# Attention steps in periods of two, and projections of the next pass on row halves, in a post-norm transformer layer on 8 cores

## The chip, the cores and the metric

The kernel runs on all 8 cores of one Trainium2 chip. The time is device microseconds of the slowest core. Before the change the median of 3 runs is 1495.09 us (1491.83 to 1698.76). Each core takes half of the query blocks of one of 4 batch entries: 2048 of 4096 tokens, in 128-token blocks that alternate between two cores. There is no communication between cores.

## The reference

One layer on x of shape (4, 4096, 1024), f32, all of it computed on the chip:

```python
x = _layernorm(x + attn(x, Wq, Wk, Wv, Wo))        # 16 heads of 64, causal softmax
x = _layernorm(x + ffn(x, w_gate, w_up, w_down))   # 3072 hidden, silu(gate) * up, int weights / 127
```

Attention is `softmax(scale * Q K^T, causal) V` for each head, with Q, K and V projected from x.

## The kernel before, in words

**Attention** takes two heads per pass, 8 passes. A core's 2048 queries are 4 banks of 512; a bank is done against the key blocks that it may see, one *step* per 128 keys (in the masked part two blocks share a step): 5, 13, 21 and 29 steps, 68 per pass and 544 in all. A step is:

- `scores` (L497): K block times Q bank for head 0 on rows 0 to 63 and head 1 on rows 64 to 127 of TensorE, into one of two buffers `sps` (two PSUM banks each). The two matmuls of such a pair run at once. They wait for the exponential of two steps before.
- the exponential (L505) on ScalarE over both heads, 128x1024, into `pt`, with the pass's bound `cbias` in place of a running maximum. `masks` (L522, L529) on VectorE multiplies the diagonal blocks.
- `values` (L553): V (with a column of ones for the row sums) times `pt`, added into `ops`, one bank per head. The 128 keys are split in two halves of 64 rows: in each *phase* the two heads take different row halves, and in the second phase they swap. Since both phases add to the same banks from different rows, phase 1 waits for phase 0 (`wait(pe, s_pe, pv_at[j])`).

The order is written out: values(j-1, 0), scores(j+2), masks(j), values(j-1, 1), then filler. At a bank's end `unit_out` copies `ops` to `ostg` (L569), and the next bank's first values wait for it; 6 steps later `unit_recip` takes the reciprocal of the row sums, with a DMA before and two behind it; 16 steps later `unit_scale` (L594) multiplies, into `ofm`. These stand in VectorE's one queue with everything else there.

**Filler** is the work of the next pass, a generator that yields its cost in units of one 512-column matmul. It has 8 groups of K (`k_group`, L260), 4 of Q (L278), each 8 matmuls of 128 rows by 512 columns into one of two PSUM banks `pp`, evacuated by VectorE; 8 groups of V (L299, 16 matmuls of 256 columns each) in passes 0 to 5; and the *bound*: squares of K and Q (L328), their column sums on TensorE with a 32-column weight (`norms`, L337), a maximum (L342), `spread` and `gather_max` (L359), then `roots` on ScalarE, which give `cbias`. Credit grows by `rate` per step, and filler is issued once 4 units are saved up (2 at a bank's end): about 5 matmuls after every second step. Groups take the two banks in turn. Pass 7 has no filler.

Before attention the projections of pass 0 run from x, which is loaded by DMA. In the first 36 x 13 steps DMAs convert the feed-forward weights to bf16 in DRAM, and in pass 7 the output weights and x are loaded (L617, L621). After attention come the output projection, layer norm, gate and up, down, and the second norm.

Of the kernel before, what the change touches and what calls it, by code (L numbers as in the profile page):

```python
# [75 lines left out]
def build_program(cfg):  # L76
# [37 lines left out]
    with st:  # L114
# [128 lines left out]

        pp_free = [0, 0]
# [71 lines left out]

        sq_free = [0]
# [60 lines left out]
        def bound(p):  # L378

            squares(p, 0)  # L380
            yield 0.5
            norms(p, 0)
            squares(p, 1)
            yield 1.5
            norms(p, 1)
            squares(p, 2)
            yield 1.5
            norms(p, 2)
            spread(p)
            yield 1.5  # L390
            gather_max(p)
            yield 0.5
            roots(p)
            yield 0.0

        def together(groups, stages):

            for g in groups:
                yield from g
                cost = next(stages, None)  # L400
                if cost is not None:
                    yield cost
            for cost in stages:
                yield cost

        def proj_kq(p):
            for ts in range(NTS):
                yield from k_group(p, ts)
                if ts % 2 == 1:
                    yield from q_group(p, ts // 2)  # L410
            if p + 2 < NPASS:
                wait(pool, s_pe, s_pe.n)
                load_wk(p + 2)
                load_wq(p + 2)

        def filler(p):

            if p + 1 >= NPASS:
                return
            v = (p + 2) // 2  # L420
            yield from proj_kq(p + 1)
            groups = []
            if 2 * v < NPASS:
                lo = 0 if p % 2 == 0 else NTS // 2
                groups = [v_group(v, ts, h) for ts in range(lo, lo + NTS // 2) for h in range(2)]
            yield from together(groups, bound(p + 1))
            if p % 2 == 1 and v + 1 < NPASS // 2:
                wait(pool, s_pe, s_pe.n)
                load_wv(v + 1)

        def filler_cost(p):
            if p + 1 >= NPASS:
                return 0.0
            cost = 12 * 8 + 5.5
            if 2 * ((p + 2) // 2) < NPASS:
                cost += 8 * 16 * 0.52
            return cost
# [18 lines left out]
        load_wq(2)  # L456
        squares(0, 1)
# [7 lines left out]
        spread(0)  # L465
        gather_max(0)
# [42 lines left out]
        def masks(j):  # L509
# [9 lines left out]
            if stride == 1:  # L519
                tv = t.rearrange("p (h q) -> p h q", h=2)[:, :, 0:128]  # L520
                mv_ = m[:, 0:256].rearrange("p (h q) -> p h q", h=2)
                s_dve.inc(dve.tensor_mul(tv, tv, mv_))  # L522
            else:
                for h in range(2):
                    n = 512 // 128
                    tv = t[:, h * 512:(h + 1) * 512].rearrange(
                        "p (b q) -> p b q", b=n)[:, 0:n:stride // 128, :]
                    mv_ = m[:, h * 256:(h + 1) * 256].rearrange("p (b q) -> p b q", b=2)
                    s_dve.inc(dve.tensor_mul(tv, tv, mv_))  # L529
            pt_at[j] = (s_dve, s_dve.n)  # L530

        def values(j, phase):
# [5 lines left out]
            if phase == 0:  # L538
# [5 lines left out]
            else:  # L544

                wait(pe, s_pe, pv_at[j])
            flip = (phase + j) % 2
            for kb, q0, w, so in s["segs"]:
                for half in range(2):
                    h = half ^ flip  # L550
# [5 lines left out]
                                   start=(s["first"] and phase == 0),  # L556
                                   stop=(s["last"] and phase == 1),
# [65 lines left out]
        work = filler(0)  # L623
        credit = [0.0]
        rate = [filler_cost(0) / 66.0]

        def fill(least):
            if credit[0] < least:
                return
            while credit[0] > 0:  # L630
                cost = next(work, None)
                if cost is None:
                    credit[0] = 0.0
                    return
                credit[0] -= cost

        scores(0)
        scores(1)
        NJ = len(plan)
        for j in range(NJ + 1):  # L640
            if j > 0:
                values(j - 1, 0)
            if j + 2 < NJ:
                s = plan[j + 2]
                if s["opens"]:
                    for _ in work:
                        pass
                    p = s["p"]
                    work = filler(p)
                    rate[0] = filler_cost(p) / 66.0  # L650
                    credit[0] = 0.0
                scores(j + 2)
            if j < NJ:
                masks(j)
            if j > 0:
                values(j - 1, 1)
                done = plan[j - 1]
                if done["last"]:
                    u = done["unit"]
                    unit_out(u, j - 1)  # L660
                    pending.append((j + 6, lambda u=u: unit_recip(u)))
                    pending.append((j + 16, lambda u=u: unit_scale(u)))
                    pending.sort(key=lambda e: e[0])
                if done["p"] < NPASS - 1:
                    if j % 13 == 12:
                        convert_piece()
                else:
                    n = j - 1 - (NJ - 68)
# [299 lines left out]
```

How the kernel before makes its waits and increments, by code:

```python
    def inc(self, instr, k=1):  # L50
        instr.then_inc(self.h, k)
        self.n += k
        return self.n
# [2 lines left out]
def wait(engine, sem, value):  # L56
    if value > 0:
        engine.wait_ge(sem.h, value)
```

## Time and profile before

| | |
|---|---|
| median of 3 runs | 1495.09 us |
| the profiled execution | 1492.57 us; span of its slowest core 1491.5 us |
| cores | 1483.7 to 1491.5 us |
| TensorE matmuls busy | 1361.2 us, 91% |
| TensorE weight loads busy | 630.2 us, 42%, beside the matmuls |
| ScalarE busy | 725.3 us, 49% |
| VectorE busy | 472.8 us, 32% |
| chain that ended last | PE 81%, DVE 5%, DMA 5%, issue 5%, ACT 4% |

Busy time is the union of an engine's instructions; matmuls are pipelined, so one's duration is longer than its distance to the next, and the distances are what tells TensorE's pace. A row of the timeline gathers like instructions that follow each other: start, time from the first start to the last end, engine, line, names, count, and in brackets the idle time before and what ended it. Since rows of one engine overlap at their ends, cost is read from one row's start to the next row's start. All times below are of the slowest core, 3, from its first instruction.

### The profile page before, as it was taken

Reading aid. Unit: us, or ns where it says so; the run is one execution under the profiler, and the core shown is the slowest. Engines: PE = TensorE matmul, PEld = TensorE weight load, DVE = VectorE, ACT = ScalarE, POOL = GpSimd, SP = SyncE. Lnnn points to the kernel's source line nnn. Section 1 sums busy time; section 2 is a strip of 40 time slices with the busy share of each in tenths; the row PEclk is TensorE's granted clock in tenths of the full one; section 3 lists DMA queues with packets and bytes.
Section 4 is the critical chain, followed back from the end, with each engine's and each line's share of the span. In section 5 each row is a group of like instructions: output and inputs, shape, how many; then the busy total and the mean of one; then the engine's idle time right before and its main releaser. Section 6 shows DMA issues by size and latency. Waiting matters only on the chain.

```text
span 1491.5 us, 23901 instructions; the slowest of 8 cores (1483.7 to 1491.5 us)
## 1 busy us (share of the span) xinstructions
PE 1361.2 (91%) x8432; PEld 630.2 (42%) x8432; DVE 472.8 (32%) x950; ACT 725.3 (49%) x809; POOL 97.8 (7%) x190
## 2 busy tenths in 40 slices
PE   5989999999999999999997687889999999999998
PEld 3634434434434444434433333334444444444443
DVE  1432333333334333332423125622231222122222
ACT  0067666766776676666786793641101121130123
POOL 2000000000000000000000110011101101100100
PEclk9999999999999999999998899999999999999999
DMA  9913113222122223221321641038304423431422
GB/s 153 152 26 50 37 35 52 44 51 51 30 51 36 53 42 51 44 36 22 54 48 30 160 137 64 1 114 268 127 15 147 153 82 114 153 130 58 154 85 99
DMA packets 38863, 119.68 MB, mean 80 GB/s; under 512 B 13280, under 2 KB 13280, under 8 KB 36576
## 3 DMA queue, kind: packets, MB, share of 16 engines
q0 software_dynamic: 24096, 100.68, 28.7%
q1 hardware_dynamic: 14656, 17.47, 3.7%
q8 instruction: 76, 1.25, 0.3%
q14 instruction: 35, 0.29, 0.1%
HBM read 145.13 MB, written 27.39 MB: 116 GB/s over the span
## 4 chain that ended last, share of the span: by engine, by line
PE 81%; DVE 5%; DMA 5%; issue 5%; ACT 4%; POOL 0%; DVEq 0%; ACTq 0%; SPq 0%; POOLq 0%
PE ops L553 20%; PE gps L816 11%; PE ups L822 11%; PE dps L876 11%; PE sps L497 7%; PE pp L260 7%; PE pp L299 7%; PE pp L278 3%; DMA xb<-xP 3%; ACT pt L505 2%; PE dps L728 2%; DVE ostg L569 2%; DMA linvd<-rcol 1%; DVE vbuf L311 1%; DMA lb<-linvd 1%
## 5 line engine op out<-in xcount | busy, mean ns | idle before, releaser
L505 ACT ACTIVATE pt<-sps,cbias 128x1024 bf16<-128x1024 f32 x544 | 575.8, 1117 | 235.2 <-PE sps L497 229.8
L553 PE MATMUL ops<-pt,vbuf 64*65 64x512 bf16 (+3 forms) x2560 | 397.9, 361 | 49.4 <-DVE ostg L569 18.7
L553 PEld LDWEIGHTS ops<-pt,vbuf 64*65 64x65 bf16 x2560 | 150.2, 106 | 297.3 <-issue 293.7
L828 ACT ACTIVATE sgb<-gps 128x512 bf16<-128x512 f32 x96 | 57.3, 597 | 371.3 <-PE gps L816 371.3
L497 PE MATMUL sps<-qbuf,kbuf 64*128 64x512 bf16 (+3 forms) x1280 | 220.2, 353 | 10.8 <-ACT pt L505 9.7
L816 PE MATMUL gps<-x1T,wgu 128*128 128x512 bf16 x768 | 183.2, 382 | 0.0
L822 PE MATMUL ups<-x1T,wgu 128*128 128x512 bf16 x768 | 181.9, 380 | 0.0
L876 PE MATMUL dps<-wd,hbuf 128*128 128x512 bf16 x768 | 166.4, 379 | 0.0
L260 PE MATMUL pp<-xb,wkb 128*128 128x512 bf16 x512 | 134.4, 391 | 19.2 <-DMA xb<-xP 18.3
L831 DVE SCALAR_TENSOR_TENSOR hbuf<-ups,sgb 128x512 bf16<-128x512 f32 x96 | 66.4, 692 | 267.3 <-PE ups L822 267.3
L299 PE MATMUL pp<-wvb,xb 128*128 128x256 bf16 x1024 | 133.2, 277 | 12.2 <-DVE vbuf L311 12.1
L299 PEld LDWEIGHTS pp<-wvb,xb 128*128 128x128 bf16 x1024 | 94.5, 99 | 47.6 <-issue 34.6
L816 PEld LDWEIGHTS gps<-x1T,wgu 128*128 128x128 bf16 x768 | 75.5, 98 | 91.3 <-issue 1.7
L822 PEld LDWEIGHTS ups<-x1T,wgu 128*128 128x128 bf16 x768 | 75.3, 98 | 91.3 <-issue 1.1
L876 PEld LDWEIGHTS dps<-wd,hbuf 128*128 128x128 bf16 x768 | 75.1, 98 | 90.6
L267 DVE CAST kbuf<-pp 128x512 bf16<-128x512 f32 x64 | 44.2, 691 | 183.9 <-PE pp L260 183.9
L497 PEld LDWEIGHTS sps<-qbuf,kbuf 64*128 64x128 bf16 x1280 | 77.0, 101 | 50.4 <-issue 41.5
L311 DVE CAST vbuf<-pp 128x512 bf16<-128x512 f32 x64 | 44.4, 694 | 168.5 <-PE pp L299 168.5
L770 POOL DMA_DIRECT2D wgu<-wgub x96 | 50.6, 528 | 492.7 <-PE ups L822 476.8
L260 PEld LDWEIGHTS pp<-xb,wkb 128*128 128x128 bf16 x512 | 43.9, 99 | 80.6 <-issue 43.9
L278 PE MATMUL pp<-xb,wqb 128*128 128x512 bf16 x256 | 68.3, 384 | 0.0
L884 DVE SCALAR_TENSOR_TENSOR x<-x,mv,dps 128x512 f32<-128x512 f32 x32 | 23.9, 748 | 114.3 <-PE dps L876 102.2
(55 smaller groups left out, 594.9 us busy)
## 6 DMA issues: line engine op xcount, KB each, us to landing
wgu<-wgub POOLq DMA_DIRECT2D x96, 512.0 KB, 4.3
wgub<-wguP POOLq DMA_DIRECT2D x24, 512.0 KB, 6.2
xb<-xP POOLq DMA_DIRECT2D x8, 1024.0 KB, 38.2
lb<-linvd SPq DMA_DIRECT2D x32, 256.0 KB, 3.7
x<-xtok POOLq DMA_DIRECT2D x16, 512.0 KB, 4.3
yout<-x SPq DMA_DIRECT2D x15, 512.0 KB, 2.7
wdb<-wdP POOLq DMA_DIRECT2D x12, 512.0 KB, 6.1
wd<-wdb POOLq DMA_DIRECT2D x6, 1024.0 KB, 8.5
```

Of the source, the lines that this page charges most:

```text
L260: mm = pe.matmul(pp[i][:, :], wkb[p % 2][:, c * 128:(c + 1) * 128], xb[ts][:, c * 512:(c + 1) * 512], start=(c == 0), stop=(c == NCH - 1))
L278: mm = pe.matmul(pp[i][:, :], wqb[p % 2][:, c * 128:(c + 1) * 128], xb[2 * g][:, c * 512:(c + 1) * 512], start=(c == 0), stop=(c == NCH - 1))
L299: mm = pe.matmul(pp[i][:, b * 256:(b + 1) * 256], xb[ts][:, c * 512 + t0:c * 512 + t0 + 128], wvb[v % 2][:, c * 256:(c + 1) * 256], start= ...
L311: s_dve.inc(dve.tensor_copy(dst, src))
L497: mm = pe.matmul(buf[:, h * 512 + so:h * 512 + so + w], kt[r, kb * 128:kb * 128 + 128], qt[r, g * 512 + q0:g * 512 + q0 + w], start=True, ...
L505: exp_at[j] = s_act.inc(act.activation(pt[j % NPT][:, :], buf[:, :], AF.Exp, bias=cbias[p % 2][:, 0:1]))
L553: mm = pe.matmul(ops[:, h * 512 + q0:h * 512 + q0 + w], vt[r, c0:c0 + 65], pt[j % NPT][r, h * 512 + so:h * 512 + so + w], start=(s["first" ...
L816: mm = pe.matmul(gps[:, :], wgu[i][:, c * 128:(c + 1) * 128], xt[:, c * 512:(c + 1) * 512], start=(c == 0), stop=(c == NCH - 1))
L822: mm = pe.matmul(ups[j][:, :], wgu[i][:, D + c * 128:D + (c + 1) * 128], xt[:, c * 512:(c + 1) * 512], start=(c == 0), stop=(c == NCH - 1))
L828: gps_free[0] = s_act.inc(act.activation(sgb[j][:, :], gps[:, :], AF.Silu, scale=QS))
L831: h_at[hc] = s_dve.inc(dve.scalar_tensor_tensor(hbuf[:, hc * 512:(hc + 1) * 512], ups[j][:, :], QS * QS, sgb[j][:, :], op0=ALU.mult, op1=A ...
L876: mm = pe.matmul(dps[i][h][:, :], hbuf[:, hc * 512 + k * 128:hc * 512 + k * 128 + 128], wd[:, hc * D + h * 512:hc * D + h * 512 + 512], st ...
```

## The change

1. *Periods of two steps.* Steps of one bank are taken two at a time. A period is: the second halves of the values of the two steps before (one wait for both), then for each of its own steps scores two ahead, mask, and the first half of its values, then filler. Which head is on which rows now depends on the period. A bank has an odd number of steps, so its last period has one.
2. *Projections on row halves.* Groups of filler go in pairs, as `kq_pair` and `v_quad`: a matmul of 128 rows becomes two of 64, one for each group (and each `pp` bank), on different rows at the same time. After 8 such pairs the groups turn: each takes the other half of its rows, and waits for the first turn. Both banks must be free before a pair of groups starts, and both are evacuated behind it. The code before the passes keeps its 128-row groups.
3. *Filler kept for bank ends.* Each bank gets its share per period, less 7.5 units, which are issued between the scores and the first values after a bank's end. Filler stops at a turn or at a group pair's end, except that at a bank's end it goes past a turn. The stages of the bound are spread over the filler at other places, and the first K pair of pass 1 is issued before `gather_max` of pass 0 (`ahead`).
4. *Masks* in the strided case are one VectorE instruction in place of two.

```diff
+        def halves(outs, lhs, rhs, turns, first, last):
+            for half in range(2):
+                n = half ^ turns
+                r = slice(64 * half, 64 * half + 64)
+                mm = pe.matmul(outs[n], lhs[n][r, :], rhs[n][r, :], start=first, stop=last)
+            return mm
+        def kq_pair(p, w, w_sem, w_value, tiles, evacuate):
+            for i in range(2):
+                wait(pe, s_dve, pp_free[i])
+                wait(pe, s_xb[tiles[i]], 16)
+            wait(pe, w_sem, w_value)
+            for turns in range(2):
+                if turns == 1:
+                    wait(pe, s_pe, flipped)
+                for c in range(NCH):
+                    wc = w[:, c * 128:(c + 1) * 128]
+                    mm = halves([pp[0][:, :], pp[1][:, :]], [wc, wc],
+                                [xb[t][:, c * 512:(c + 1) * 512] for t in tiles],
+                                turns, turns == 0 and c == 0, turns == 1 and c == NCH - 1)
...
+                                wait(dve, s_pe, flipped)
+                                pp_free[i] = evacuate(i)
+                    yield 1.0
+                yield FLIP if turns == 0 else DONE
...
+        def v_quad(v, ts):
...
+            for b, turns in ((0, 0), (0, 1), (1, 1), (1, 0)):
+                opening = (b == turns)
+                if not opening:
+                    wait(pe, s_pe, flipped)
...
+        def fill(least, over_flips=False):
+            if credit[0] < least:
+                return
+            while credit[0] > 0:
+                cost = next(work, None)
...
+                if cost > 0:
+                    credit[0] -= cost
+                elif cost == DONE or not over_flips:
+                    return
...
         spread(0)
+        ahead()
         gather_max(0)
...
+        for n, now in enumerate(periods):
+            heads = n % 2
+            if before:
+
+                wait(pe, s_pe, pv_at[before[-1]])
+            for j in before:
+                values(j, 1, heads)
+                finished(j)
...
+                share = max(0.0, rate[0] * steps - AT_END) / ((steps + 1) // 2)
+            for j in now:
+                look_ahead(j + 2)
                 masks(j)
+                if plan[j]["first"] and j > 0:
+                    credit[0] += AT_END
+                    fill(0.1, over_flips=True)
+                values(j, 0, heads)
+                settle(j)
+            credit[0] += share
+            fill(1.0)
+            before = now
```

TensorE's order in pass 0, in its fourth bank, where V is the filler (`ops` are values, `sps` scores, `wvb` the V weights; the number behind `pt` is the buffer, so the step). Before:

```order
L299 MATMUL pp<-wvb_73,xb_45 128x256 x9
L553 MATMUL ops<-pt_96,vbuf_80 65x512 x2
L497 MATMUL sps<-qbuf_78,kbuf_76 128x512 x2
L553 MATMUL ops<-pt_96,vbuf_80 65x512 x2
L553 MATMUL ops<-pt_97,vbuf_80 65x512 x2
L497 MATMUL sps<-qbuf_78,kbuf_76 128x512 x2
L553 MATMUL ops<-pt_97,vbuf_80 65x512 x2
L299 MATMUL pp<-wvb_73,xb_45 128x256 x7
```

Now, in the same bank:

```order
L324 MATMUL pp<-wvb_73,xb_45 128x256 x16
L640 MATMUL ops<-pt_98,vbuf_80 65x512 x2
L640 MATMUL ops<-pt_95,vbuf_80 65x512 x2
L592 MATMUL sps<-qbuf_78,kbuf_76 128x512 x2
L640 MATMUL ops<-pt_96,vbuf_80 65x512 x2
L592 MATMUL sps<-qbuf_78,kbuf_76 128x512 x2
L640 MATMUL ops<-pt_97,vbuf_80 65x512 x2
L324 MATMUL pp<-wvb_73,xb_46 128x256 x16
```

The two halves of one step, which stood on either side of one scores, now have the filler between them; the second halves of two steps stand together. A filler row of 16 is 8 pairs.

TensorE's order at the end of the third bank of pass 0 (the last step is the one of 256-column values). Before:

```order
L278 MATMUL pp<-xb_49,wqb_71 128x512
L299 MATMUL pp<-wvb_73,xb_43 128x256 x7
L553 MATMUL ops<-pt_97,vbuf_80 65x256 x4
L497 MATMUL sps<-qbuf_78,kbuf_76 128x512 x2
L553 MATMUL ops<-pt_97,vbuf_80 65x256 x4
L299 MATMUL pp<-wvb_73,xb_43 128x256 x5
L553 MATMUL ops<-pt_98,vbuf_80 65x512 x2
L497 MATMUL sps<-qbuf_78,kbuf_76 128x512 x2
```

Now:

```order
L592 MATMUL sps<-qbuf_78,kbuf_76 128x512 x2
L640 MATMUL ops<-pt_97,vbuf_80 65x256 x4
L324 MATMUL pp<-wvb_73,xb_43 128x256 x16
L640 MATMUL ops<-pt_97,vbuf_80 65x256 x4
L592 MATMUL sps<-qbuf_78,kbuf_76 128x512 x2
L324 MATMUL pp<-wvb_73,xb_43 128x256 x26
L640 MATMUL ops<-pt_98,vbuf_80 65x512 x2
L592 MATMUL sps<-qbuf_78,kbuf_76 128x512 x2
```

Between the bank's last values and the next bank's first stood 5 matmuls of 256 columns; now there are one scores pair and 13 pairs of 256 columns. The first values stand ahead of the scores in the one, and behind one of them in the other.

## Rows read from the trace of the kernel before

**Rows 1.** Cores: span and mean granted clock, the slowest and the fastest.
```profile
core 3: 1491.5 us, clock 0.977
core 4: 1483.7 us, clock 0.980
```

**Rows 2.** Busy time by stretch; from 78.10 on one row for a pass.
```profile
78.10:181.70 103.60, 97.86 (x700) 43.98 (x700) 34.13 (x74) 72.43 (x70) 3.58 (x7) 0.97 0.21 34
...
288.50:394.60 106.10, 98.98 (x721) 45.03 (x718) 37.67 (x82) 72.77 (x71) 3.89 (x8) 0.98 0.26 46
...
711.50:808.10 96.60, 83.97 (x590) 35.92 (x586) 32.44 (x73) 71.57 (x71) 2.58 (x5) 0.96 0.22 40
808.10:893.50 85.40, 62.19 (x480) 30.33 (x482) 19.07 (x50) 69.76 (x68) 10.60 (x20) 0.88 0.53 137
893.50:1491.50 598.00, 567.95 (x2704) 258.95 (x2704) 172.04 (x295) 145.86 (x249) 53.74 (x102) 0.98 0.33 110
```

**Rows 3.** Groups by line: busy us, mean ns, then idle before.
```profile
L267 DVE CAST kbuf<-pp 128x512 bf16<-128x512 f32 x64 | 44.2, 691 | 183.9 <-PE pp L260 183.9
...
L569 DVE COPY ostg<-ops 65x1024 f32<-65x1024 f32 x32 | 39.0, 1220 | 40.5 <-PE ops L553 40.5
```

**Rows 4.** Timeline, pass 2, one period of two steps, without weight loads.
```profile
305.70 2.12 ACT L505 ACTIVATE pt<-sps,cbias 128x1024 bf16<-128x1024 f32 x2 [0.72 <-PE sps L497]
...
306.31 0.41 PE L553 MATMUL ops<-pt,vbuf 64*65 64x512 bf16 x2
306.65 1.25 PE L260 MATMUL pp<-xb,wkb 128*128 128x512 bf16 x5
307.83 0.41 PE L553 MATMUL ops<-pt,vbuf 64*65 64x512 bf16 x2
308.07 0.38 PE L497 MATMUL sps<-qbuf,kbuf 64*128 64x512 bf16 x2
308.39 0.62 PE L553 MATMUL ops<-pt,vbuf 64*65 64x512 bf16 x4
308.56 2.12 ACT L505 ACTIVATE pt<-sps,cbias 128x1024 bf16<-128x1024 f32 x2 [0.73 <-PE sps L497]
308.82 0.41 PE L497 MATMUL sps<-qbuf,kbuf 64*128 64x512 bf16 x2
```

**Rows 5.** Waits of PE and of ACT in pass 2 (288.5 to 394.6): us, times, longest.
```profile
PE ops L553 <- DVE ostg L569: 2.4, 2, 1.6
PE pp L299 <- DVE vbuf L311: 1.9, 2, 1.0
PE ops L553 <- DVE pt L522: 1.9, 2, 1.6
...
ACT pt L505 <- PE sps L497: 33.1, 37, 2.7
```

**Rows 6.** Timeline at the start of attention.
```profile
74.92 0.68 DVE L342 TENSOR_REDUCE red<-pp 128x1 f32<-128x512 f32 x1
...
76.48 0.36 PE L359 MATMUL pp<-e,onesf 128*128 128x8 f32 x2 [1.95 <-DVE e L353]
```

**Rows 7.** Timeline, V as filler, and norms with what follows.
```profile
142.95 1.16 PE L299 MATMUL pp<-wvb,xb 128*128 128x256 bf16 x9
144.04 0.41 PE L553 MATMUL ops<-pt,vbuf 64*65 64x512 bf16 x2
...
254.05 0.40 PE L337 MATMUL pp<-sq,onesb 128*32 128x512 bf16 x4
...
255.37 0.70 PE L299 MATMUL pp<-wvb,xb 128*128 128x256 bf16 x5 [0.92 <-DVE vbuf L311]
```

**Rows 8.** Pass 7: two exponentials at half clock; VectorE's longest DMA wait.
```profile
845.62 1.11 ACT L505 ACTIVATE pt<-sps,cbias 128x1024 bf16<-128x1024 f32 x1 [0.17 <-PE sps L497]
...
846.90 1.11 ACT L505 ACTIVATE pt<-sps,cbias 128x1024 bf16<-128x1024 f32 x1 [0.17 <-PE sps L497]
...
DVE ofm L594 <- DMA lb<-linvd: 16.1, 2, 9.8
```

More of the change, by code:

```diff
@@ L376, in roots @@
                 op0=ALU.mult, op1=ALU.mult))
[L378 to L414, printed above, removed]
         def filler(p):
-            if p + 1 >= NPASS:
+            n = p + 1
+            if n >= NPASS:
                 return
             v = (p + 2) // 2
-            yield from proj_kq(p + 1)
-            groups = []
+            yield from k_pair(n, 0)
@@ new lines, in filler @@
+            yield from k_pair(n, 1)
+            yield from q_pair(n, 0)
+            squares(n, 0)
+            yield from k_pair(n, 2)
+            norms(n, 0)
+            yield 0.8
+            yield from k_pair(n, 3)
+            squares(n, 1)
+            yield from q_pair(n, 1)
+            if n + 2 < NPASS:
+                wait(pool, s_pe, s_pe.n)
+                load_wk(n + 2)
+                load_wq(n + 2)
+            norms(n, 1)
+            squares(n, 2)
+            yield 0.8
+            tiles = []
@@ L423, in filler, with values_of @@
             if 2 * v < NPASS:
                 lo = 0 if p % 2 == 0 else NTS // 2
-                groups = [v_group(v, ts, h) for ts in range(lo, lo + NTS // 2) for h in range(2)]
-            yield from together(groups, bound(p + 1))
+                tiles = list(range(lo, lo + NTS // 2))
+            def values_of():
+                if tiles:
+                    yield from v_quad(v, tiles.pop(0))
+            yield from values_of()
+            norms(n, 2)
+            spread(n)
+            yield 0.8
@@ L427, in filler @@
+            yield from values_of()
+            gather_max(n)
+            yield 0.3
+            yield from values_of()
+            roots(n)
+            yield from values_of()
             if p % 2 == 1 and v + 1 < NPASS // 2:
@@ L621, in x1_load, with look_ahead @@
             s_x1[t // 4].inc(pool.dma_start(x1[t][:, :], xtok[t * 128:(t + 1) * 128, :]), 16)
[L623 to L628, printed above, removed]
-                return
[L630 to L635, printed above, removed]
+        def look_ahead(j):
+            nonlocal work
+            if j >= NJ:
+                return
+            s = plan[j]
+            if s["opens"] and j > 0:
+                for _ in work:
+                    pass
+                p = s["p"]
+                work = filler(p)
+                rate[0] = filler_cost(p) / 67.0
+                credit[0] = 0.0
+            scores(j)
```

149 lines of the change are left out of this document (94 added, 55 removed).

## The prediction

> **What bounds the kernel now.** I read the views in this order: cores, busy time by pass, groups of instructions, one stretch of attention on the timeline, then the waits of that pass.
>
> The cores agree within half a per cent, so one core tells the story [rows 1]. The busy time by stretch [rows 2] has one row for each pass of attention between its first exponentials: pass 0, pass 2 (which stands for passes 1 to 5: together 711.5 - 181.7 = 529.8 us, 106 each), pass 6, pass 7. In pass 2 TensorE is busy 99 of 106 us, ScalarE 73. ScalarE has 68 exponentials per pass; two in a row take 2.12 us [rows 4], so a pass can't be shorter than 68 x 1.06 = 72 us. In passes 1 to 6 it waits for scores (33.1 us in pass 2 alone [rows 5]): TensorE sets the time there, by its own order, since few of its waits name another engine [rows 5]. Pass 7 has no filler (the next pass's projections), and is 85.4 us.
>
> Where TensorE's time goes is seen in one period of two steps [rows 4]. In the row of four values matmuls at 308.39, two pairs take 0.43 us until the scores at 308.82: a pair of 64-row matmuls over 512 columns costs 0.215 us, the same as one 128-row matmul. From there:
> - Values, first half at 307.83, scores 308.07, second half 308.39: 0.56 us for two pairs, 0.13 more than streaming. The second half writes the same banks from the other rows, and waits for the first.
> - Values at 306.31 to projection at 306.65: 0.34 us, 0.125 more than a pair. Five projection matmuls from 306.65 to 307.83: 1.18 us, 0.105 more than 5 x 0.215. So a stretch of filler costs 0.23 us beyond its work.
> - Together 11 x 0.215 + 2 x 0.13 + 0.23 = 2.86 us, which is the distance of the two ScalarE rows (305.70 to 308.56). ScalarE idles 0.73 of it.
>
> A pass of 106.1 us is then: 204 step pairs, 96 units of K and Q, 64 of V (128 matmuls of half width) and about 3 for norms, 367 x 0.215 = 78.9; 68 x 0.13 = 8.8; the order of before has 36 stretches of filler per pass, 36 x 0.23 = 8.3; the other 10.1 are waits (6.2 in [rows 5], the rest mostly around the norms).
>
> **The change, part by part.**
> *Second halves in twos.* 68 waits per pass become about 34, and with filler between first and second halves the wait is over before it is reached. Where no filler stands between (some 4 periods per pass), it is exposed: 0.56 - 0.215 = 0.35 us. Saved: 8.8 us less 1.4.
> *Projections on row halves.* Twice the instructions, in pairs that share time; no change between 128-row and 64-row work but for norms and the gather: 4 x 0.23 = 0.9 in place of 8.3. That a projection pair costs 0.215 is taken from the scores and values pairs [rows 4]. For 256 columns: nine 128-row V matmuls take 1.09 us to the next values, less 0.105 is 0.11 each [rows 7]; half a 512 pair is 0.108, and I take that. No stretch of before has more than a few pairs of halves in a row; the new ones have up to 16. Bounds: 0.215 (no loss; two halves can't be shorter than their columns) to 0.43 (one after the other).
> The Trainium skill, "TensorE: Matmul & The Clock Gate", section "Measured speedup vs the span model", gives 3.07x for four row tiles at 512 columns, where full overlap would be 4x. Rows 4 don't bear this out for two. By the page's ratio each new pair would cost 1.3 times as much; that is a rival below.
> *Turns.* Each group pair turns its halves once, and waits for its first turn. The filler mostly stops there, and other work covers it. At bank ends it goes on: 3 or 4 times per pass x 0.35 = 1.4 us.
> *Both banks per group.* A group pair starts only when both pp banks are evacuated: 0.41 us to the last matmul's end and 2 x 0.69 on VectorE [rows 3, 4], about 1.75 us, against 6 x 0.215 = 1.3 us at least of values and scores between two fillers. Bounds nothing to 1.5 us for each of 10 groups; most periods are 2.1 us or more, so I take 0.2, 2.0 in all, and 1.3 at the pass's seam, where the flushed last group is followed at once by the next pass's first.
> *Norms.* From the norms to the next V matmul 1.32 us pass (254.05 to 255.37 [rows 7]), 1.1 beyond their own 0.22 (the four stand in separate column strips, and their row is as long as one matmul); after, the next group needs that bank too. I keep 3 x 1.1 = 3.3.
> *Bank ends.* 7.5 units of filler (1.6 us) between the last scores and the first values cover the 1.22 us copy [rows 3]: the 2.4 us of waits in [rows 5] go. The masks, now one instruction in place of two, made TensorE wait 1.9 us in the unstrided case. Both waits are taken as zero after; their bound above is what they are now, 4.3.
> *Filler in uneven pieces.* ScalarE has two buffers. From the second scores of a period it has 2.12 us of work; less 0.49 from scores to exponential (308.07 to 308.56) and four pairs (0.86), TensorE may spend 0.77 us, about 4 units, on filler. The order of after has pieces of 5 and 3, 6 and 2, 7 and 1, or 8 and none: the long piece starves ScalarE, and in the short one TensorE waits for ScalarE. 0.2 to 0.6 us per two periods, 16 of these: 6 us, which before did not exist.
> Pass 1 to 5 after: 78.9 + 0.9 + 1.4 + 1.4 + 3.3 + 3.3 + 6 = 95.2; some waits fall together, so 94. Over five passes 470 against 529.8: **-59.8**.
> *Start.* The first group pair now runs before the gather of pass 0. It starts when the last reduction is done (75.6 [rows 6]), takes 16 x 0.215 + 0.35 = 3.8, its end and two evacuations another 1.8, so the gather moves from 76.48 to about 81.3: **+4.8**. Bounds -0.5 (the clock, which falls to half in this stretch before, stays up) to +6. In return pass 0 has 16 units less: 94 - 3.4 = 90.6 against 103.6: **-13.0**.
> *Pass 6*, no V: TensorE has 303 units = 65 us, so ScalarE's 72 bound, plus 4 bank ends of 1.2 (8 units between two scores), plus 5 for the bound's chain: 82 against 96.6, **-14.6**.
> *Pass 7*: no filler before or after. It holds a DMA stall (VectorE waits 16.1 us for lb, 9.8 of them at once [rows 8], and masks queue behind it); that stays. At the half clock level a step costs 1.28 us (845.62 to 846.90 [rows 8]), three pairs; the period's exposed wait adds a little: **+0.6**.
> After attention nothing changes: 598 us [rows 2].
> Sum: +4.8 - 13.0 - 59.8 - 14.6 + 0.6 = -82.0. The profiled execution took 1492.6 us (span 1491.5), 2.5 under the median of 1495.1: 1492.6 - 82.0 = **1411 us**.
>
> What is late next: TensorE still (about 86 of 94 us), with ScalarE 73; both within a fifth of each other, so pieces and buffers matter more than before.
>
> **Rivals.**
> *A, the two pp banks become the wait.* VectorE is in order; a bank copy (1.22), two scales or squares ahead of the evacuations push them back. If each of the 10 groups waits 0.8 instead of 0.2: 0.6 x 10 x 7 = 42 us, 1453. For: before, two banks alternated and still gave 1.9 us of waits in pass 2 [rows 5]. Against: VectorE is busy 38 of 106 us [rows 2].
> *B, long runs of pairs lose pace,* some 30% per pair: K and Q pairs 7 x 96 = 672 x 0.065 = 44 us, V pairs 768 x 0.032 = 25: 1411 + 69 = 1480, no measurable change. For: the trace has no long run of them. Against: [rows 4] show no loss at two. (This is also what the page's ratio gives.)
> *C, halves run one after the other* in the projections, because two weight loads and two matmuls a pair don't overlap in a sustained run: 672 x 0.215 + 768 x 0.108 = 227 us, 1638, slower. From half of that loss on (111 us) the kernel is over 2% slower. Against: the values pairs in [rows 4].
> *D, waits and uneven pieces hide in each other:* 89 in passes 1 to 5, 86 in pass 0, 78 in pass 6: 34 us less, 1377. For: ScalarE's slack and the waits for pp come in the same short periods. Against: the norms wait comes ahead of long pieces.
>
> **Numbers.** Forecast 0.60, A 0.14, D 0.12, B 0.09, C 0.05. The range takes in D and A: 1375 to 1455. Two per cent (30 us, about what a measurement of this kernel tells from no change) is 1465: faster is forecast, A and D, 0.86; same B, 0.09; slower C, 0.05.
>
> **What would show it.** Distance of ScalarE rows in an even period: 2.15 to 2.4 us for two steps, from 2.86. Passes 1 to 5 near 94; ScalarE's wait for scores in pass 2 near 22 us. Projection pairs 0.215 apart and V pairs 0.108; if 0.28 or 0.43, B or C holds. TensorE's wait for kbuf, qbuf or vbuf evacuations under 3 us per pass, or A holds. First exponential near 83 us. Pass 7 within 5 us of 85. Most at risk is the 6 us for uneven pieces, since no row of before shows such a period, and the DMA stall, which comes at another moment in faster passes.

## The result, and the profile after

The kernel after takes **1503.87 us** (median of 8 runs, 1497.94 to 1614.21) beside 1494.71 us of the kernel before. The ratio is **1.0054**, 95% interval 1.003 to 1.0078: half a per cent slower, where 1411 us was forecast. In three of the eight runs, the profiled one among them, cores of one die ran longer at a lower granted clock; the median of the other five is 1501.1 us (before: 1493.1), and the times below are medians without such runs.

```profile
core: us from the first to the last instruction, mean granted TensorE clock
core 0: 1524.8 us, clock 0.949
core 3: 1492.2 us, clock 0.972
die 1 (median of its cores): 1495.9 us, clock 0.972
```

These are lines of the view of the cores of after, for [rows 1]. Cores 0 and 1 lost some 30 us behind attention, where their granted clock was 0.81 for 162 us, so what follows is read on core 3, the core of the rows of before. On core 3 the two traces differ by 0.7 us only (1491.5 and 1492.2), since it is the slowest core of before and one of the fastest of after: the cores of before take 1483.7 to 1491.5 us, cores 2 to 7 of after 1491.6 to 1499.4. So core 3 shows some 7 us less of a loss than the medians, which is little beside the 83 us by which it is over the forecast. Its busy time by stretch, for [rows 2] (columns as there): pass 0, pass 1, pass 2, pass 6, pass 7, and what follows attention.

```profile
81.30:178.30 97.00, 84.06 (x888) 50.08 (x888) 31.32 (x61) 71.94 (x70) 3.58 (x7) 0.96 0.21 37
178.30:289.10 110.80, 92.76 (x946) 55.51 (x946) 38.12 (x74) 72.27 (x70) 3.55 (x7) 0.95 0.29 44
289.10:395.60 106.50, 90.42 (x945) 53.47 (x942) 36.39 (x70) 72.36 (x71) 4.12 (x8) 0.97 0.31 46
712.80:808.30 95.50, 78.88 (x688) 39.22 (x685) 31.62 (x61) 71.55 (x70) 2.58 (x5) 0.95 0.21 40
808.30:890.90 82.60, 60.47 (x482) 27.60 (x482) 17.96 (x36) 70.32 (x69) 10.58 (x20) 0.94 0.54 141
890.90:1492.20 601.30, 569.32 (x2704) 259.49 (x2704) 171.84 (x294) 145.74 (x248) 53.74 (x102) 0.98 0.33 109
```

| stretch, us | before | forecast | after |
|---|---|---|---|
| start, to the first exponential | 78.1 | 82.9 | 81.3 |
| pass 0 | 103.6 | 90.6 | 97.0 |
| passes 1 to 5 together | 529.8 | 470 | 534.5 |
| pass 6 | 96.6 | 82 | 95.5 |
| pass 7 | 85.4 | 86.0 | 82.6 |
| behind attention | 598.0 | 598.0 | 601.3 |

So the miss is in the passes with filler: 6.4 + 64.5 + 13.5 us. TensorE is busy less in pass 2 (90 us for 99), and the pass isn't shorter: the saving is there, and is given back as waits. Where, the waits of pass 2 tell, for [rows 5] (smaller ones left out):

```profile
PE ops L640 <- DVE pt L620: 5.7, 5, 1.2
PE pp L324 <- DVE rcol L665: 2.6, 2, 2.1
PE sps L592 <- ACT pt L600: 2.4, 7, 0.4
PE pp L324 <- DVE red L430: 1.4, 1, 1.4
PE pp L324 <- DVE red L422: 1.2, 1, 1.2
ACT pt L600 <- PE sps L592: 34.6, 32, 3.7
```

The wait for `ostg` at bank ends is gone, as forecast. But the first values wait 5.7 us for masks (L620; 2.3 before, 1.9 of it in [rows 5]), the scores wait for ScalarE, and filler waits 5.2 us for VectorE's last instruction before the second `pp` bank comes free (`rcol` and `red` are only what stood last in its queue). ScalarE waits for scores as long as before.

Three stretches of pass 2 on the timeline, for [rows 4]; rows between those shown are left out. First, two pieces of filler.

```profile
306.23 1.25 PE L324 MATMUL pp<-xb,wqb 64*128 64x512 bf16 x10 [0.43 <-DVE rcol L665]
307.31 0.61 PE L640 MATMUL ops<-pt,vbuf 64*65 64x512 bf16 x4
308.23 4.13 ACT L600 ACTIVATE pt<-sps,cbias 128x1024 bf16<-128x1024 f32 x4 [0.89 <-PE sps L592]
308.60 0.83 PE L324 MATMUL pp<-xb,wqb 64*128 64x512 bf16 x6
309.25 0.61 PE L640 MATMUL ops<-pt,vbuf 64*65 64x512 bf16 x4
310.49 0.39 PE L592 MATMUL sps<-qbuf,kbuf 64*128 64x512 bf16 x2 [0.20 <-ACT pt L600]
```

Ten halves take 1.08 us to the next values, 0.216 a pair, and six take 0.65, so nothing is added where they end. The 0.43 us in front of the ten is the wait for the second bank. Pieces of 5 and 3 units follow each other. Behind the 5, ScalarE has idled 0.89 us; behind the 3, TensorE waits for ScalarE.

Next, masks of a bank's end, with VectorE's queue.

```profile
315.49 0.42 DVE L620 TENSOR_TENSOR pt<-pt,mk 128x512 bf16<-128x512 bf16 x1
315.82 1.39 DVE L681 TENSOR_TENSOR ofm<-ostg,lb 64x512 bf16<-64x512 f32 x2
316.05 0.41 PE L640 MATMUL ops<-pt,vbuf 64*65 64x384 bf16 x4 [1.23 <-DVE pt L620]
316.77 1.11 ACT L600 ACTIVATE pt<-sps,cbias 128x1024 bf16<-128x1024 f32 x1 [0.73 <-PE sps L592]
317.24 0.76 DVE L620 TENSOR_TENSOR pt<-pt,mk 128x512 bf16<-128x512 bf16 x2
317.81 1.83 PE L640 MATMUL ops<-pt,vbuf 64*65 64x384 bf16 x12 [1.14 <-DVE pt L620]
320.17 1.11 ACT L600 ACTIVATE pt<-sps,cbias 128x1024 bf16<-128x1024 f32 x1 [2.28 <-PE sps L592]
```

A period's second mask stands in VectorE's one queue behind the two scales of `unit_scale` (1.39 us), and the masked values behind it on TensorE; then ScalarE gets no scores for 2.28 us. The granted clock is 0.5 from 317.9 to 321.3, so the rows there are longer by the clock too. Last, the norms, for [rows 7].

```profile
327.12 1.39 DVE L681 TENSOR_TENSOR ofm<-ostg,lb 64x512 bf16<-64x512 f32 x2
327.27 0.40 PE L417 MATMUL pp<-sq,onesb 128*32 128x512 bf16 x4
328.54 0.69 DVE L422 TENSOR_REDUCE red<-pp 128x1 f32<-128x512 f32 x1
329.80 1.47 PE L324 MATMUL pp<-xb,wkb 64*128 64x512 bf16 x12 [2.13 <-DVE rcol L665]
```

From norms to the next group pair it is 2.53 us, since that pair needs the bank that the norms used, and their maximum waits behind the scales too; the other two of this pass take 1.57 us (350.94 to 352.51) and 1.77 (361.54 to 363.31).

### The profile page after: what moved, and what is told of

Read it like the earlier page. It is cut to its first block, busy times and chain, and to the rows that moved or that the text cites. A ratio compares the mean times of both kernels' runs of the same rounds, so it can differ in the third digit from the quotient of the medians.

```text
span 1524.8 us, 26429 instructions; the slowest of 8 cores (1491.6 to 1524.8 us)
## 1 busy us (share of the span) xinstructions
PE 1335.2 (88%) x9872; PEld 689.6 (45%) x9872; DVE 463.9 (30%) x854; ACT 723.0 (47%) x809; POOL 97.8 (6%) x190
## 4 chain that ended last, share of the span: by engine, by line
PE 71%; ACT 10%; issue 8%; DVE 7%; DMA 4%; DVEq 0%; POOL 0%; ACTq 0%; SPq 0%; POOLq 0%
PE pp L324 15%; PE gps L921 12%; PE ups L927 12%; PE dps L981 11%; PE ops L640 11%; ACT pt L600 9%; PE sps L592 6%; PE dps L833 2%; DMA xb<-xP 2%; PE pp L300 1%; DVE red L422 1%; DMA linvd<-rcol 1%; DVE kbuf L352 1%; DVE pt L620 1%; DVE ofm L681 1%
## 5 line engine op out<-in xcount | busy, mean ns | idle before, releaser
L592 PE MATMUL sps<-qbuf,kbuf 64*128 64x512 bf16 (+3 forms) x1280 | 223.0, 356 | 23.6 <-ACT pt L600 23.2
L921 PE MATMUL gps<-x1T,wgu 128*128 128x512 bf16 x768 | 193.4, 398 | 0.0
L927 PE MATMUL ups<-x1T,wgu 128*128 128x512 bf16 x768 | 191.8, 395 | 0.0
L981 PE MATMUL dps<-wd,hbuf 128*128 128x512 bf16 x768 | 175.4, 393 | 0.0
L324 PE MATMUL pp<-xb,wkb 64*128 64x512 bf16 x896 | 126.3, 398 | 20.2 <-DVE rcol L665 13.3
L324 PE MATMUL pp<-wvb,xb 64*128 64x256 bf16 x1536 | 103.8, 274 | 22.9 <-DVE red L430 8.1
L921 PEld LDWEIGHTS gps<-x1T,wgu 128*128 128x128 bf16 x768 | 77.9, 101 | 98.9 <-issue 34.3
L927 PEld LDWEIGHTS ups<-x1T,wgu 128*128 128x128 bf16 x768 | 77.6, 101 | 98.8 <-issue 33.5
L620 DVE TENSOR_TENSOR pt<-pt,mk 128x512 bf16<-128x512 bf16 (+1 forms) x160 | 56.1, 367 | 151.5 <-ACT pt L600 150.8
L324 PEld LDWEIGHTS pp<-wvb,xb 64*128 64x128 bf16 x1536 | 83.7, 95 | 39.7 <-issue 30.8
L324 PEld LDWEIGHTS pp<-xb,wkb 64*128 64x128 bf16 x896 | 50.6, 99 | 67.6 <-issue 40.1
L656 DVE COPY ostg<-ops 65x1024 f32<-65x1024 f32 x32 | 39.1, 1221 | 88.0 <-PE ops L640 83.8
L389 DVE CAST vbuf<-pp 128x512 bf16<-128x512 f32 x48 | 31.0, 688 | 105.8 <-PE pp L324 105.8
```

The lines of the kernel that those rows point to most:

```text
L324: mm = pe.matmul(outs[n], lhs[n][r, :], rhs[n][r, :], start=first, stop=last)
L592: mm = pe.matmul(buf[:, h * 512 + so:h * 512 + so + w], kt[r, kb * 128:kb * 128 + 128], qt[r, g * 512 + q0:g * 512 + q0 + w], start=True, ...
L921: mm = pe.matmul(gps[:, :], wgu[i][:, c * 128:(c + 1) * 128], xt[:, c * 512:(c + 1) * 512], start=(c == 0), stop=(c == NCH - 1))
L927: mm = pe.matmul(ups[j][:, :], wgu[i][:, D + c * 128:D + (c + 1) * 128], xt[:, c * 512:(c + 1) * 512], start=(c == 0), stop=(c == NCH - 1))
L981: mm = pe.matmul(dps[i][h][:, :], hbuf[:, hc * 512 + k * 128:hc * 512 + k * 128 + 128], wd[:, hc * D + h * 512:hc * D + h * 512 + 512], st ...
```

## The experiments

Times are medians in us; the ratio is to the kernel before run in the same batch, with its 95% interval. Two theories on the 83 us by which core 3 is over the forecast: **U**, filler that stops at every turn comes in uneven pieces and costs far more than the 6 us a pass of the forecast; **M**, masks, norms and both `pp` banks put VectorE's queue in TensorE's way. "Half clock" is time in attention on core 3 at a granted clock of 0.5 (1.2 of 2.4 GHz): before 47 us, after 58. Waits without a pass named are those of core 3 in all of attention.

**Masks left out**, in after and in before.

```diff
-            if s["mask"] is None:
+            if True:
```

> The changed kernel with the masks on the exponentials left out, so its result isn't causal there; it does no other work. Theory M (the gain was lost to the masks, since the first half of a step's values now stands right behind the scores that the exponential released, so the time of exponential, mask and semaphore is open on TensorE, and the halts let the granted clock fall): passes 1 to 5 from about 106 to about 98, span shorter by 45 to 70 us, half clock in attention back to 40 us or less. Rival R1 (halves in pairs, the turns or the pp banks cost it): under 15 us. Rival R2 (the masks cost as much before; they aren't what the change added): the same saving as in the kernel before without masks.

> The kernel before with the masks left out, as the control for the run above. Theory M: 10 to 25 us shorter than before (TensorE waited 26 us for masks over the whole kernel, part of it in the DMA stall of pass 7). Rival R2: as much as in the changed kernel, 45 us or more.

1447.48, ratio 0.971 (0.968 to 0.974), and 1480.13, 0.992 (0.989 to 0.995). Masks cost after 54 us (1501.1 - 1447.5) and before 12 (1491.7 in the same batch - 1480.1), as M had it; R1 and R2 fall. They are not free in after; and even without them it is 36 us over the forecast, with passes 1 to 5 at 100.6 us for 94 and pass 6 at 88.0 for 82. Half clock is 41 us there.

**Filler stops behind norms; filler split** over both steps of a period; both.

```diff
             norms(n, 0)
             yield 0.8
+            yield DONE
```
```diff
+                else:
+                    credit[0] += share / (len(now) + 1)
+                    fill(0.1)
                 values(j, 0, heads)
```

> The changed kernel; the filler stops for the period behind each norms, spread and gather, instead of going on at once with a group that needs the bank just used. Theory N (a part of the loss is the wait of the next group for both banks behind norms, 1.3 to 2.3 us three times a pass): 15 to 30 us shorter than the changed kernel. Rival: the filler not issued there is issued in longer pieces later and ScalarE starves then; within 8 us.

> The changed kernel with the share of filler of a period issued in three pieces (between mask and first half of values of each of its two steps, and at the end) instead of one. Theory M: the pieces before the first halves cover most of the mask's time, 30 to 55 us shorter than the changed kernel, and the waits of ops for pt fall from 45 us to under 15. Rival (uneven pieces starving ScalarE are the larger part): ScalarE's wait for scores falls also in unmasked stretches. If neither holds, within 10 us of the changed kernel.

> The filler stop behind the norms and the filler in three pieces, together. If the two losses are separate: 35 to 45 us shorter than the changed kernel (27 and 10 alone). If the pieces again run into evacuations: no better than the stop alone, 27.

1473.07 (0.988, 0.985 to 0.991); 1492.63 (1.001, 0.998 to 1.004); 1477.54 (0.989, 0.987 to 0.992). With a period's work between the norms and the next group pair, 28 us come back: TensorE's waits for `pp` banks fall from 46 to 8 us, though those for masks rise from 45 to 60. The split brought 9 us and not the 30 to 55 expected of it, and together with the stop it is no better than the stop alone: in its trace the waits for masks fall to 32 us only, and those for `pp` banks rise from 46 to 68, in 89 pieces of filler in pass 2 for 37.

**One half of the change alone.** First the new filler in the old order of steps, then the periods of after with the old filler (128-row groups, which never stop).

> Only the filler part of the change: pairs on row halves, group pairs, turns, the new places of the bound and the first K pair ahead of the gather, with the step order of before (one step at a time, values of the step before on either side of the scores). Theory M+N: the 8 us per pass of changes between 128-row and 64-row work go, masks stay as hidden as before, the norms cost 2 us more per pass: passes 1 to 5 near 100, 30 to 45 us shorter than before. Rival R1 (halves in pairs, turns or both pp banks eat their own gain): within 15 us of before.

> Only the step order of the change (periods of two, one wait for the second halves, filler kept for bank ends) with the 128-row filler of before. Theory M+N: the 8 us per pass of waits between halves go, but 5 to 7 us of open masks come, plus the clock: within 15 us of before, and slower than the run above by 20 us or more. Rival (the periods are the good part): 25 us or more shorter than before.

New filler, old order: 1486.11 (0.996, 0.994 to 0.998), 7 us under before and not 30 to 45, passes near 103.9. It isn't a clean test of the price of row halves: its pieces are uneven too (5 and 3, 7 and 1), and TensorE waits 60 us for `pp` banks where before has 18. Periods, old filler (e6): **1431.7 (0.959, 0.957 to 0.961)**, 61 us under before and 69 under after. The expectation, within 15 us of before, fell: this is the faster kernel of the three. It has the filler kept for bank ends and the masks in one instruction as well, so the 61 us aren't of the second halves alone. Its pass 2 and a period in it:

```profile
270.20:365.40 95.20, 90.86 (x723) 42.13 (x720) 37.03 (x70) 72.89 (x72) 3.56 (x7) 1.00 0.34 51
```
```profile
304.73 2.12 ACT L603 ACTIVATE pt<-sps,cbias 128x1024 bf16<-128x1024 f32 x2 [0.83 <-PE sps L595]
304.90 0.38 PE L643 MATMUL ops<-pt,vbuf 64*65 64x512 bf16 x2
305.21 1.04 PE L279 MATMUL pp<-xb,wqb 128*128 128x512 bf16 x4
306.18 0.62 PE L643 MATMUL ops<-pt,vbuf 64*65 64x512 bf16 x4
307.12 2.12 ACT L603 ACTIVATE pt<-sps,cbias 128x1024 bf16<-128x1024 f32 x2 [0.27 <-PE sps L595]
```

Two steps in 2.39 us, four units in this period (3 to 4.5 in most), ScalarE idle 0.27: it still pays 0.1 in front of the projections (0.31 us from values to them) and 0.11 where the four end (0.97 us to the next values), and TensorE waits for nothing here. Waits for masks are 1.8 us in this pass, half clock in all of attention 23 us.

**Uneven pieces in that kernel.** Nothing else is changed:

```diff
-            credit[0] += share
+            credit[0] += share * (1.6 if heads else 0.4)
```

> The kernel with periods of two and the 128-row filler of before (the run that took 1432 us), but each period's share of filler alternates between 0.4 and 1.6 of its value, so that pieces are 2 and 6 to 7 units, as in the changed kernel, instead of 4 and 4. No row halves, no turns. Theory U (uneven pieces are what ate the gain: after a short piece TensorE is early, runs into ScalarE and into the masks; after a long one ScalarE starves): 35 to 60 us slower than with even pieces, 1467 to 1492, with more waits of ops for pt and more time at half clock. Rival T (the pairs on row halves themselves, their turns or both pp banks are the cost): within 15 us of 1432.

1488.9 (0.998, 0.997 to 0.999): **57 us** for unevenness alone. The waits of the whole run on TensorE; with even pieces the same two are 23.2 and 7.6 us:

```profile
PE ops L643 <- DVE pt L623: 29.6, 36, 6.0
PE sps L595 <- ACT pt L603: 26.9, 96, 2.0
```

U holds for this kernel: after short pieces TensorE waits for ScalarE (19 us more), long ones starve ScalarE (its waits for scores in attention are 233 us for 168), and the two don't cancel. The waits for masks grow by 6 us only, and half clock is 27 us for 23, so neither is the main part here.

**Even pieces on row halves.** Groups rewritten so that each full period gets exactly 4 units (half a group pair) and a bank's end 8; the stages of the bound are issued after a whole group pair.

```diff
+            if len(now) == 2:
+                credit[0] += full[0]
+                fill()
```

> The changed kernel, pairs on row halves and all, but each two-step period gets exactly 4 units of filler (2 in pass 6), each bank's end 8, the single step none, so that every piece ends at a turn or in its middle and no pending turn ends a fill early; norms stay at the start of a piece. Theory U: 40 to 70 us shorter than the changed kernel, 1435 to 1460, waits of ops for pt under 25 us. Rival T: within 15 us of the changed kernel's 1500.

> As the run before, and the norms and the gather go between the first half of values of a period's first step and the next scores, so that their reduction is done when the next group pair starts. If the norms' waits (some 5 us a pass) are apart from the evenness: 20 to 30 us shorter than with even pieces alone, 1410 to 1435, at or under the 1432 of the periods alone. If they hid in ScalarE's time: within 8 us of even pieces alone.

The first (e11) takes 1474.7, lowest run 1473.34, ratio 0.988 (0.986 to 0.991): **26 us** under after, and not 40 to 70. Both expectations missed: it is more than T allows and less than U asks, and the waits for masks did not fall to under 25 us.

```profile
PE ops L660 <- DVE pt L640: 48.7, 36, 4.5
```

They are 45.4 in after. So it isn't the uneven pieces that bring the masked values up before their masks. With the norms moved to the middle of the period as well (the second kernel) the ratio is 1.004 (0.997 to 1.011), its lowest run 1488.95, and half clock rises to 72 us: a move against the expectation. The waits for masks rise to 62 us there; why was not tried.

**Masks first in VectorE's queue.** Both masks of a period ahead of all else that the period gives VectorE, scales last: in after with the stop behind the norms and 2 units of filler more before masked values; in the even kernel; in the periods with old filler. The line that moves the scales (`settle`) behind both steps isn't shown.

```diff
-                masks(j)
+                if j == now[0]:
+                    for i in now:
+                        masks(i)
```

> The stop behind the norms; both masks of a period stand ahead of its evacuations in VectorE's queue and the scaling of a unit behind them; 2 units of filler stand between the scores and the first half of the values of each masked step, and are taken from the periods' shares. Theory M: the waits of ops for pt fall from 60 us in the run with the stop alone to under 25, and the span by 25 to 45 us more than with the stop alone, near 1435. Rival (TensorE's waits for masks only stand where it would have waited for ScalarE): near 1465.

> Pairs on row halves in even pieces (1473 us), with both masks of a period put into VectorE's queue at its start, and the scaling of a unit behind both steps. If VectorE's queue is why the masks cost more here (b): waits of ops for pt from 47 to under 25 us, span 15 to 30 us shorter, near 1450. If it is TensorE's earliness alone (a) or the banks (c): within 8 us of 1473.

> Periods with 128-row filler (1432 us), with the same new order of VectorE's queue. (b): 5 to 15 us shorter, since its waits for pt are 23 us, of which 5 in one DMA stall. Otherwise within 5 us.

1448.73 (0.970, 0.969 to 0.972), 24 us under the stop alone, with waits for masks of 16.5 us for 60; 1457.35 (0.977, 0.976 to 0.979), 17 us under the even kernel, though its waits for masks are still 40.6 us and not under 25; 0.967 (0.961 to 0.973) with a lowest run of 1431.07, the same as without (1430.96). So VectorE's order is worth 17 us with filler on row halves, and nothing in the kernel with the old filler. Why it matters in the one only is not shown; in the one evacuations come in twos (1.29 us together), in the other one by one (0.69).

**Masks left out of both even kernels.**

> Pairs on row halves in even pieces, masks left out (the result isn't causal). (a) or (b): 40 to 50 us shorter than with masks, 1425 to 1433, close to the next run. (c): 20 us or less, 1453 and more, and 30 us above the next run.

> Periods with 128-row filler, masks left out (the result isn't causal). All theories: 10 to 20 us shorter than 1432. What counts is the difference to the run before: under 10 us for (a) or (b), about 30 for (c).

1428.37 (0.958, 0.956 to 0.960), 46 us under its base; lowest 1407.36 (0.949, 0.942 to 0.955), 24 us under the lowest of its base. Of the 42 us between the lowest runs of the even kernel on row halves (1473.3) and of the one with the old filler (1431.0), 22 go with the masks and 21 don't (1428.0 and 1407.4). That lies between what (a) or (b) and (c) expected.

**Norms, or both banks?** Norms of passes 1 to 7 are left out of the even kernel with masks first and of the periods with old filler; and one wait is added to the latter.

```diff
         def next_pp():
             i = pp_turn[0] % 2
             pp_turn[0] += 1
+            if i == 0 and plan_on[0]:
+                wait(pe, s_dve, pp_free[1])
             return i
```

> e13_even_masks_first (row-half filler in exact pieces of 4 units, masks first; 1457.4 us) with the norms of passes 1 to 7 left out: their matmuls over the squares and the maximum behind them aren't computed, so the exponentials' bound of those passes is that of pass 0; the squares stay. Of the 41 us by which exact pieces on row halves (e11, 1473) stay behind the 128-row filler (e6, 1432), about 20 go with masks. Theory N, the rest is the norms: they need a pp bank just as the next group pair needs both, three times per pass. Then this kernel gains 30 to 35 us, to about 1425, and e19 only 10 to 14, to about 1420. Rival B, the rest is that every group pair waits for both pp banks, norms or not: this gains 10 to 15 us only, to about 1445, and stays 20 us or more behind e19.

> e6_periods_only (periods of after with the 128-row filler; 1431.8 us) with the norms of passes 1 to 7 left out as in e18. 21 norms at their own 0.22 us plus two mode changes of 0.12 each are 9 to 10 us, a little clock more: 1418 to 1422 by both theories. The difference e18 minus e19 is what counts: near 5 us by theory N, 20 or more by rival B.

> e6_periods_only (1431.8 us) with one wait more: every second group of filler (and of the norms) in the passes starts only when both pp banks are evacuated, not only its own. The last evacuation is then behind the last matmul: 0.41 us to its end and 0.69 for the copy, 1.1 us, unless values and scores of a period stand between the groups. Rival B: the wait is paid at about half of the 10 to 12 places of each of 7 passes, 0.4 to 0.6 us each, and each pays in clock too: 1447 to 1455. Theory N: groups of 8 units end where pieces of about 4 end, so a period's own work hides it: 1432 to 1438.

1425.1 (0.955, 0.953 to 0.957), 32 us less, with half clock at 20 us for 41; 1412.94 (0.950, 0.943 to 0.958), 19 less. The two are 12 us apart, between what N (near 5) and B (20 or more) expected. With the wait: **1501.6** (1.006, 1.004 to 1.008), 70 us more. In its trace the wait stands inside pieces, where no step's work covers it:

```profile
307.78 0.82 PE L264 MATMUL pp<-xb,wkb 128*128 128x512 bf16 x3
309.90 0.38 PE L264 MATMUL pp<-xb,wkb 128*128 128x512 bf16 x1 [1.30 <-DVE rcol L672]
310.21 0.62 PE L647 MATMUL ops<-pt,vbuf 64*65 64x512 bf16 x4
```

Neither expectation had this: groups end where periods don't, so such waits, seven of them and 9.1 us in pass 2, are paid in full. Filler that needs both banks in the middle of a piece loses up to 70 us by it; after avoids that by stops, and there the stops make the pieces uneven. (The even kernel shows that stops and even pieces go together.) The norms count 13 us more on row halves (32 - 19). What is left between the two kernels without norms, 12 us in the medians (8.7 on core 3), is by their traces the start (81.3 for 75.9 us, the group pair ahead of the gather) and pass 6 (91.0 for 85.0 us); passes 1 to 5 differ by 0.7 us each, and pass 7 goes the other way.

First exponential and passes on core 3, from its exponentials (pass 7 to the last one's start, so some 1 us shorter than in the windows):

| kernel | start | 0 | 1 | 2 | 3 | 4 | 5 | 6 | 7 | half clock |
|---|---|---|---|---|---|---|---|---|---|---|
| before | 78.1 | 103.6 | 106.8 | 106.1 | 104.7 | 105.9 | 106.3 | 96.7 | 84.3 | 47 |
| after | 81.3 | 97.0 | 110.8 | 106.5 | 105.0 | 105.3 | 106.9 | 95.5 | 81.4 | 58 |
| even, row halves | 81.6 | 97.3 | 100.2 | 102.0 | 102.2 | 102.2 | 100.3 | 97.2 | 87.7 | 51 |
| and masks first | 81.4 | 98.9 | 100.1 | 98.7 | 98.9 | 99.4 | 98.8 | 93.3 | 81.4 | 41 |
| periods, old filler | 77.4 | 96.9 | 96.0 | 95.2 | 95.4 | 95.4 | 95.1 | 91.5 | 83.5 | 23 |
| and both-bank wait | 78.0 | 106.1 | 108.5 | 106.4 | 107.0 | 108.0 | 106.3 | 95.5 | 85.1 | 40 |

## Why the prediction was wrong

The prices of single instructions were right. **The step that failed** is the one in *Bank ends* by which TensorE's waits for masks are "taken as zero after": they became 45 us, and leaving the masks out of the changed kernel takes 54 us off, the larger part of the 90 us between 1411 and 1501. The 36 us that are left have several parts, of which the norms and the clock are seen in the traces, and not all of it is explained.

From after to the periods with old filler the steps are 1501.1, 1474.7, 1457.4, 1431.7: 26 us for pieces, 17 for VectorE's order, 26 for norms (13) and, by the two kernels without norms, the start and pass 6 (12).

- *Second halves in twos*: right as far as is known. It was given 7.4 us a pass, 59 in eight, and the periods with the old filler take 61 off. How the 61 divide between the second halves, the filler at bank ends (waits for `ostg` fall from 18.7 to 5.1 us) and the masks in one instruction was not tried.
- *Projections on row halves*: the price held, 0.216 a pair (1.08 us for ten halves), so rivals B and C fell; for V, eight pairs of 256 columns took 0.87 us (row below, of the even kernel with masks first: 375.40 to 376.27), 0.109 each.

```profile
375.40 1.06 PE L324 MATMUL pp<-wvb,xb 64*128 64x256 bf16 x16
376.27 0.62 PE L660 MATMUL ops<-pt,vbuf 64*65 64x512 bf16 x4
```

  The mode changes went too. In the old order of steps this was worth 7 us in all, not the 52 that 8.3 less 0.9 us a pass comes to: TensorE's waits for `pp` banks are 42 us longer there (60 for 18), about as much as is missing.
- *Bank ends*: the copy of `ostg` is hidden, as said. "Both waits are taken as zero after" was wrong for the masks: TensorE's waits for them went from 26 us (13.1 + 12.8) in the whole run to the 45.4 in the row below, and leaving the masks out gives 54 us and not 12. The reason given, one instruction in place of two, doesn't bear on the 1.9 us that it set to zero: these are of L522, the unstrided case, which had one instruction before. The wait had been short by the old order: between a mask and its values TensorE had the second halves of the step before and, every second time, a piece of filler. Now the values are TensorE's next work behind the scores, and 1.39 us of scales can stand ahead of the mask. Two units of filler put in between again, with the masks first in VectorE's queue, take the waits for masks from 60 to 16.5 us. By the runs without masks they cost 12 us in before, 24 in the new order with old filler, 46 in even pieces on row halves, of which VectorE's order gives 17 back; the rest of that difference is not explained.

```profile
PE ops L640 <- DVE pt L620: 45.4, 36, 5.7
```

- *Filler in uneven pieces*: the price was not too low for this kernel. It was given 6 us a pass, 36 in passes 0 to 5, and taking the unevenness out of after gives 26 back. In the kernel with old filler it costs 57; why twice as much is open. So it was rightly named as most at risk, but is not what made the miss.
- *Both banks per group, and norms*: each was given 3.3 us a pass, some 45 us together with the 5 of pass 6, and TensorE's waits in front of what it writes to `pp` are 46 us in after. That the sum came out is luck, since in pass 2 the norms take 5.2 us beyond their own 0.22 (2.53, 1.57 and 1.77 us to the next group, for 1.32 each) and the other groups 1.6. So rival A, 0.8 us a group, fell: the stops hide the second bank. Where the wait stands inside pieces, the added wait shows its price, 70 us. Norms as a whole count 32 us on row halves and 19 with the old filler, stalls and clock with them.
- *Clock*: the sums were made at full speed. Half clock went from 47 to 58 us in attention; the periods with old filler have 23. At most half of it is lost time, so the rise is worth at most 6 us to before, and the 58 at most 29 to the forecast. It doesn't follow the sum of the waits: it is 27 us in the kernel with uneven pieces and 68 in the one with the stop, which has the longest waits for masks of the two (60 us for 30).
- *Start*: +3.2 for +4.8. The group pair began at 74.22 and the gather at 79.71, for the forecast 75.6 and 81.3.

```profile
74.22 3.96 PE L324 MATMUL pp<-xb,wkb 64*128 64x512 bf16 x32 [1.64 <-DVE red L430]
79.71 0.36 PE L439 MATMUL pp<-e,onesf 128*128 128x8 f32 x2 [1.54 <-DVE kbuf L352]
```

- *Pass 6*: 95.5 for 82. It has filler for less than 3 units a period in groups that still stop at turns. Even the periods with old filler need 91.5 us, so ScalarE's bound of 72 plus 10 was too low a sum. Masks left out of after bring it to 88.0, norms left out of the periods with old filler to 85.0. What fills the rest was not tried.

The range, 1375 to 1455, holds the periods with old filler and not the change itself. "What is late next: TensorE still" was a thought that misled: TensorE is busy 90 of 106 us in pass 2 and ScalarE 72, so neither is late by itself, and their order is.

## What to carry to other kernels

When two engines are both some three quarters busy or more and are joined by two buffers, price a change of order by the longest and the shortest piece of work between two hand-overs and by what stands in the third engine's queue at that moment; the sum of busy time does not show it. A faster form of background work that needs more buffers at once, or can only stop at few places, may be worth less than its slower form that can stop anywhere: here the periods with 128-row filler (1431.7 us) beat both kernels, and putting the two-bank wait into them cost all of it. Before costing a wait at nothing because the work in its cover is long enough, look whether the cover will still stand in front of it once the order changes: the masks' wait was small before because of what stood there, and was the largest part of what was missed. And when a run in one kernel shows that something is dear (57 us for uneven pieces), take it out of the kernel in question too (26 us) before calling it the cause.

## What was not expected of the hardware

Two matmuls on different row halves keep their full overlap over long runs: 0.216 us a pair of 512 columns in runs of 3 to 8, 0.109 at 256. The turn costs what it was priced at if nothing stands in between: the 16 pairs from 74.22 take 3.96 us, which is 16 x 0.215, 0.18 for the end of the last, and 0.34. Changing between 128-row and 64-row work costs about 0.1 us each way and stays the smaller evil: the fastest kernel that computes all of the reference pays both once in nearly every period.
